# A fused four-part token kernel: products of the output experts turned round, factors spread over partitions by DMA, inverse roots by one power

## The reference, cut to what matters

```python
x = layernorm(x + A(x))   # Mamba block: conv over 4 taps, SSM over 4 heads, RMS norm, out_proj, LayerNorm
x = layernorm(x + B(x))   # attention of 8 heads; values and outputs come from one of 8 experts per head and token
x = layernorm(x + C(x))   # linear attention of 16 heads, gelu, rotary turn of q and k, LayerNorm
x = layernorm(x + D(x))   # soft mixture of 64 experts over all 4096 tokens
```

```python
values = einsum('bhne,ehdk,bnd->bhnk', gm, value_experts, x)
out    = einsum('bhij,bhjk->bhik', softmax(masked q k^T), values)
out    = einsum('bhne,ehkd,bhnk->bhnd', gm, output_experts, out).sum(heads)
```

## Time and profile before

| what | value |
|---|---|
| median of 3 runs | 1497.77 us (1497.28 to 1497.99) |
| profiled execution: its own time / its span | 1495.65 us / 1493.8 us |
| busy: TensorE (PE) / VectorE (DVE) / ScalarE (ACT) / GpSimd (POOL) | 1434.7 / 1205.2 / 820.6 / 748.6 us |
| mean granted TensorE clock | 0.98 |
| start of the first slot (block 2's `a_seg`) | 103.4 us |
| first instruction of D | 1005.5 us |

### The profile page before, as it was taken

The page is one execution under the profiler, slowest core; times in us unless marked ns, Lnnn a source line. Parts: engine busy times, 40 slices in busy tenths (PEclk is TensorE's granted clock), DMA queues, the critical chain, the costliest instruction groups (busy, mean ns, idle before and its releaser), DMA issues. The chain is left out here.

```text
span 1493.8 us, 32591 instructions
## 1 busy us (share of the span) xinstructions
PE 1434.7 (96%) x10940; PEld 1267.7 (85%) x10940; DVE 1205.2 (81%) x2359; ACT 820.6 (55%) x1850; POOL 748.6 (50%) x1833
## 2 busy tenths in 40 slices
PE   8789999999999999999999999988999999898998
PEld 6658888888888888888888887867999999898998
DVE  6778889889888898898898887768888888757664
ACT  4354555454555464455555544306776777667775
POOL 1433346346355354454453451226777777467772
PEclk8889999999999999999999999998999999999999
DMA  5100000000000000000000004007777777887872
GB/s 194 61 8 8 1 15 2 14 16 1 15 15 2 16 5 12 15 5 12 16 1 15 8 1 128 2 3 174 196 193 193 191 192 195 264 315 297 312 304 75
DMA packets 135426, 130.43 MB, mean 87 GB/s; under 512 B 7232, under 2 KB 125248, under 8 KB 128768
## 3 DMA queue, kind: packets, MB, share of 16 engines
q1 hardware_dynamic: 135296, 128.79, 27.9%
HBM read 72.93 MB, written 55.84 MB: 86 GB/s over the span
## 5 line engine op out<-in xcount | busy, mean ns | idle before, releaser
L737 PE MATMUL ps_l<-ve_f,oe 128*128 128x128 f32 x2048 | 275.7, 279 | 0.8 <-DVE ve_f L1740 0.8
L737 PEld LDWEIGHTS ps_l<-ve_f,oe 128*128 128x128 f32 x2048 | 248.8, 192 | 23.1 <-issue 20.4
L1740 DVE SCALAR_TENSOR_TENSOR ve_f<-ps_s,oT 128x512 f32<-128x512 f32 x248 | 166.7, 681 | 4.1 <-PE ps_l L737 2.3
L2934 POOL TENSOR_TENSOR d_s<-d_ex 128x1024 f32<-128x1024 f32 x31 | 125.2, 4040 | 83.0 <-ACT d_ex L2684 82.8
L1701 DVE COPY_PREDICATED vals<-oh,ps_l 128x1024 f32<-128x1024 int32 x112 | 146.9, 1312 | 19.3 <-PE ps_l L477 17.4
L2559 PE MATMUL ps_s<-d_ex,arena 128*128 128x128 f32 x1024 | 121.1, 277 | 4.6 <-DVE d_ex L2827 4.6
L2559 PEld LDWEIGHTS ps_s<-d_ex,arena 128*128 128x128 f32 x1024 | 118.2, 194 | 5.0 <-DVE d_ex L2827 5.0
L2547 PE MATMUL ps_l<-arena 128*128 (+1 forms) x960 | 114.5, 279 | 3.9 <-ACT d_raw L2679 3.9
L1293 ACT ACTIVATE ve_f<-ps_l,r 128x128 f32<-128x128 f32 x128 | 47.3, 370 | 125.9 <-DVE r L1713 125.6
L2547 PEld LDWEIGHTS ps_l<-arena 128*128 128x128 f32 x960 | 111.9, 195 | 4.1 <-ACT d_raw L2679 4.1
L475 PE MATMUL ps_l<-veH,x1H 128*128 128x512 f32 x256 | 115.2, 450 | 0.1
(11 more groups left out here) (332 smaller groups left out, 3842.7 us busy)
## 6 DMA issues: line engine op xcount, KB each, us to landing
logits<-d_raw SPq DMA_DIRECT2D x128, 256.0 KB, 3.5
e_lt<-logits SPq DMA_DIRECT2D x32, 1024.0 KB, 5.1
y_slots<-d_ys SPq DMA_DIRECT2D x64, 256.0 KB, 4.6
d_ex<-y_slots SPq DMA_DIRECT2D x8, 1024.0 KB, 6.9
e_y<-y_slots SPq DMA_DIRECT2D x6, 1024.0 KB, 7.2
d_w<-W SPq DMA_DIRECT2D x16, 256.0 KB, 3.4
arena<-xT SPq DMA_DIRECT2D x16, 128.0 KB, 2.4
arena<-x SPq DMA_DIRECT2D x16, 128.0 KB, 2.4
```

Source lines behind the costliest of these rows:

```text
L737: last = pe.matmul(ps_u[:, cols], oe[:, hp, e, :], mo[:, n % MO, hp, :], start=False, stop=(e == NE - 1 and hp == HP - 1), skip_group_chec ...
L1740: V.scalar_tensor_tensor(mo[:, n % MO, :, :].rearrange("p a n -> p (a n)"), chosen_of(b, c), float(NE - e), oT[:, u, c, :, :].rearrange("p ...
L2934: G.tensor_tensor(s8[:], part[:, 0:8, :], part[:, 8:16, :], ALU.add).then_inc(n, 1)
```

## The change

It rearranges B and C's turn and roots; D stays. In words: (1) the output product has `mo` as weights and `oe` as moving operand, so its sum has tokens on partitions, in `ps_m`, and `b_oa`, `b_oat` go; `b_start` becomes four products. (2) Expert numbers and factors of a block (32 values a token) are transposed once (`b_rnt`), copied (`b_rn`), stored to DRAM and read back spread over 64 partitions twice (`spread`); `b_choice`, `b_oht`, `b_rgs`, `b_rgb`, `b_ot` times factor go; ACT copies `ps_o` to `oT` twice a block, and one 128x1024 multiplication on DVE (`b_og`) puts the factors in. `b_mo` now reads the numbers from SBUF. (3) `c_rot` is two DMAs (`swap`) for blocks 0 to 12; the sign sits in `sinT`. (4) Roots on GpSimd are one scale-and-add and one power. (5) Scores of two head pairs are made at once in two PSUM tiles. (6) All engines' orders are new.

```diff
+def root(pool, wait_apart, done, k, source, var, eps, half, v, y):
+    wait_apart(pool, source)
+    pool.tensor_scalar(v[:], var, 1.0, eps, ALU.mult, ALU.add).then_inc(done, 1)
+    wait_apart(pool, (done, k + 1))
+    pool.tensor_tensor(y[:], v[:], half[:], ALU.pow).then_inc(done, RSQRT_OPS - 1)
...
+            def spread(b):
+                sp.wait_ge(q["b_rn"], b + 1)
+                wait(sp, q["b_nb"], 32 * (b - 1))
+                sp.dma_start(rn_dram[b % 2].rearrange("a r n -> (a r) n"), rows_s[0:4 * C * HP, :]
+                             ).then_inc(q["b_rn_out"], 16)
+                sp.wait_ge(q["b_rn_out"], 16 * (b + 1))
+                wait(sp, q["b_mo"], OUTS * b)
+                for a in range(2):
+                    sp.dma_start(nb[DH * a:DH * (a + 1), :, :, :, :].rearrange("p q c h n -> p (q c h n)"),
+                                 rn_dram[b % 2, a:a + 1].rearrange("a r n -> a (r n)").to_broadcast([DH, 2 * C * HP * P])
+                                 ).then_inc(q["b_nb"], 16)
+            def swap(b):
+                sp.wait_ge(q["c_q"], b + 1)
+                wait(sp, q["c_qr"], 2 * b)
+                sp.dma_start(t1[0:P:2, :, :], ql[1:P:2, :, :]).then_inc(q["c_swap"], 16)
+                sp.dma_start(t1[1:P:2, :, :], ql[0:P:2, :, :]).then_inc(q["c_swap"], 16)
...
                 for u in range(2):
+                    spread(2 * pair + u - 2)
                     load(2 * pair + u + 1, 1 - u)
+                    swap(2 * pair + u - 3)
                     store(2 * pair + u - 3)
...
                 for n in range(3):
                     sp.wait_ge(held_in[n], 16)
+            spread(Z)
...
+            def b_rnt(b):
+                pe.wait_ge(q["b_rg"], 2 * (b + 1))
+                wait(pe, q["c_x3t"], b - 1)
+                pe.transpose(mixed_home(b)[0:4 * C * HP, 0:P], mixed_of(b), id_f[:]).then_inc(q["b_rn_ps"], 1)
...
             def b_start(b, u):
-                wait(pe, q["b_v"], (NE - 1) * capped(b + 2))
-                pe.matmul(ps_u, id_r[:], x1H[:, u, :], start=True, stop=False, skip_group_check=True)
-                pe.matmul(ps_u, id_r[:], x1L[:, u, :], start=False, stop=False,
-                          skip_group_check=True).then_inc(q["b_start"], 1)
+                wait(pe, norms["lnB"]["rows"], C * b)
+                for c in range(C):
+                    cols = slice(c * P, (c + 1) * P)
+                    pe.matmul(sum_of(b)[:, cols], x1H[:, u, cols], id_r[:], start=(c == 0), stop=False,
+                              skip_group_check=True)
+                    last = pe.matmul(sum_of(b)[:, cols], x1L[:, u, cols], id_r[:], start=False, stop=False,
+                                     skip_group_check=True)
...
-                    last = pe.matmul(ps_u[:, cols], oe[:, hp, e, :], mo[:, n % MO, hp, :], start=False,
+                    last = pe.matmul(sum_of(b)[:, cols], mo[:, n % MO, hp, :], oe[:, hp, e, :], start=False,
...
+            def b_rn(b):
+                act.wait_ge(q["b_rn_ps"], b + 1)
+                wait(act, q["b_rn_out"], 16 * b)
+                copy(rows_s[0:4 * C * HP, :], mixed_home(b)[0:4 * C * HP, 0:P]).then_inc(q["b_rn"], 1)
+            def b_ot(b, u, g):
+                act.wait_ge(q["b_pv"], 2 * b + g + 1)
+                wait(act, q["b_mo"], OUTS * (b - 1))
+                copy(oT[:, u, :, 2 * g:2 * g + 2, :].rearrange("p c h n -> p h c n"),
+                     ps_o.rearrange("p (h c n) -> p h c n", h=2, c=C)).then_inc(q["b_ot"], 1)
...
+            def b_og(b, u):
+                dve.wait_ge(q["b_nb"], 32 * (b + 1))
+                dve.wait_ge(q["b_ot"], 2 * (b + 1))
+                V.tensor_tensor(oT[:, u, :, :, :], oT[:, u, :, :, :], nb[:, 0, :, :, :], ALU.mult).then_inc(q["b_og"], 1)
...
-                V.scalar_tensor_tensor(mo[:, n % MO, :, :].rearrange("p a n -> p (a n)"), chosen_of(b, c), float(NE - e),
+                V.scalar_tensor_tensor(mo[:, n % MO, :, :].rearrange("p a n -> p (a n)"),
+                                       nb[:, 1, c, :, :].rearrange("p a n -> p (a n)"), float(NE - e),
```

More of the change, by code:

```diff
@@ L329, in token_blocks @@
             a_op_ps a_r a_xb a_n a_x1t_ps a_x1h a_x1l a_x1
-            b_g_ps b_eg b_gate b_oht_ps b_oht b_qk_ps b_qk b_v_ps b_v0 b_v b_vg b_s_ps b_max b_p b_pt_ps b_pt
-            b_pv b_rg b_rgs b_rgb_ps b_rgb b_ot b_m_ps b_mo b_oe b_oa b_oat_ps b_x2t_ps b_x2t b_start
-            c_qk_ps c_g c_km c_q c_v_ps c_v c_rot_ps c_qr c_t2 c_krt_ps c_kr c_kv_ps c_kv c_out_ps c_z c_res c_n
+            b_g_ps b_eg b_gate b_qk_ps b_qk b_v_ps b_v0 b_v b_vg b_s_ps b_max b_p b_pt_ps b_pt
+            b_pv b_rg b_rn_ps b_rn b_rn_out b_nb b_ot b_og b_mo b_oe b_x2t_ps b_x2t b_start
+            c_qk_ps c_g c_km c_q c_v_ps c_v c_swap c_qr c_t2 c_krt_ps c_kr c_kv_ps c_kv c_out_ps c_z c_res c_n
             c_x3t_ps c_x3t c_x3""".split()
@@ L448, in _ @@
             sp.dma_start(oe[:], o_exp).then_inc(experts_in, 16)
-            for b in range(2, 5):
-                load(b, b % 2)
+            load(2, 0)
+            load(3, 1)
+            spread(0)
+            load(4, 0)
+            spread(1)
+            swap(0)
             store(0)
@@ L709, in b_choice @@
-            def b_choice(b, u, c):
-                if c == 0:
-                    pe.wait_ge(q["b_oht"], b + 1)
-                if (b, c) != (Z, 1):
-                    wait(pe, q["b_mo"], OUTS * b + NE * c)
-                else:
-                    wait(pe, q["b_pt"], HB * NB)
-                rows = slice(64 * c, 64 * c + 64)
-                for hp in range(HP):
-                    last = pe.matmul(chosen_of(b, c)[:, hp * P:(hp + 1) * P], pick[rows, hp, :, :].rearrange("p a k -> p (a k)"),
-                                     ohT[rows, u, :], start=True, stop=True, skip_group_check=True)
-                last.then_inc(q["b_m_ps"], 1)
@@ L1169, in _ @@
                     logits_ahead(k, i)
-            awake(ps_a, 14)
+            b_x2t(Y, 0)
+            c_qk(Y, 0)
+            b_start(Z, 1)
+            c_v(Y, 0)
+            b_out(Z, 0, 0)
+            b_out(Z, 0, 1)
+            c_rot(Y)
+            b_out(Z, 0, 2)
+            b_out(Z, 0, 3)
+            c_krt(Y)
+            b_out(Z, 0, 4)
+            b_out(Z, 0, 5)
+            c_kv(Y)
+            b_out(Z, 0, 6)
+            b_out(Z, 0, 7)
+            c_out(Y)
+            b_out(Z, 1, 0)
+            b_out(Z, 1, 1)
+            b_out(Z, 1, 2)
+            b_out(Z, 1, 3)
+            b_out(Z, 1, 4)
+            b_out(Z, 1, 5)
+            b_out(Z, 1, 6)
+            b_out(Z, 1, 7)
+            awake(ps_a, 20)
             b_x2t(Z, 1)
             c_qk(Z, 1)
-            awake(ps_a, 6)
+            c_x3t(Y)
+            for k in range(BK - 1):
+                logits_ahead(k, BB - 1)
             c_v(Z, 1)
@@ L2108, in _ @@
             b_v(1, 4)
-            b_mo(0, 0, 0, 1)
+            b_og(0, 0)
+            b_mo(0, 0, 0, 0)
             b_v(1, 5)
@@ L2157, in _ @@
             slot(NB // 2, 0, False, True, True, True, False)
+            b_res(Y)
+            b_x2(Y, 0)
+            b_og(Z, 1)
             b_mo(Z, 1, 0, 0)
@@ L2199, in _ @@
             G = nc.gpsimd
+            G.memset(half[:], -0.5)
             def a_am(b):
```

816 lines of the change are left out of this document (320 added, 496 removed).

## The result

The changed kernel takes **1442.09 us** (median of 4 runs, 1439.58 to 1445.82) against 1497.53 of the kernel before (4 runs); the ratio is 0.9634, 95% interval 0.9611 to 0.9658. I had forecast 1461, range 1444 to 1484: faster, as I said, but by 55 us where I had 37, and just outside the range. The profiled execution took 1441.11 us, with a span of 1439.4.

A forecast was written before the change was run, and what follows sets the result against it. PE was taken to bound the slots, latencies the head and tail. From 1495.65 us: slots 3 to 14 -29, slots 15 and 16 -5, head -8, tail +5, together -37, 1458.7; plus 2.1 for the median, 1461 us, range 1444 to 1484.

The forecast's parts named there:

- the sign: Whole kernel: forecast to become faster, chance 0.89, against 0.03 for the same and 0.08 for slower.
- 2.9 us priced for groups removed and added: PE in a slot: 3.1 us of factors, choice, `b_oht`, `b_oat` and `c_rot` leave, `b_rnt` comes; net 2.9 us off.
- the new wait of PE that I charged: PE in the values' section, through `b_og` and the spread's reads: 0.5 us of new idle a slot, bounds 0 and 2.
- slots 15, 16 and tail: End of the blocks before D: two slots save 2.4 us each, about 5, and the tail grows by 5, bounds 0 and +9.
- Two banks for scores and longer runs of `b_out`: PE's order within a slot: may save a few tenths of a us, counted as nothing.
- my rule: PE's groups: each priced by the distance from its first start to the next group's start, such as 0.33 us a choice.
- The head: Start to 158 us: 8 us less, from 3.1 for the root, 2 for block 1, 3 for block 0; bounds -13 and -2.
- "Nothing in the slots" for the roots: GpSimd's roots in the slots: they end long before their use, so shortening them frees GpSimd and nothing else.
- 1 (DVE the bound): Values' section: DVE becomes the bound, idle 1.5 to 2 us a slot instead of 0.5, about 1479 us; chance 0.16.
- 2 (late read): Spread's reads take 12.2 us, `b_og` 6 us late, 4 us a slot not absorbed, 1519 us; chance 0.08.
- 3 (GpSimd and DVE hold each other): Slots: DVE's two-SBUF-input work holds GpSimd, `a_mx` and `b_vg` slip 1 to 2 us, near 1475 us; chance 0.06.
- 4 (nothing waits, 1450): Whole kernel: no new idle, the clock holds, tail +2, 1450 us; chance 0.12.

## Why the prediction was right, and where it failed

**Right.** PE as the bound of the slots and the sign; 2.7 of the 2.9 us priced for groups removed and added; `b_rnt` 0.11 and `b_start` 0.58 us; the exchange of operands at nothing; `b_mo` at 0.69; no DVE wait for `ln2` in the head; 11.3 us from `b_rnt(Z)` to `b_out(Z)` (I had 10).

**Right by luck.** `b_og` at +12.2 us of the slot (I had +12.3): the reads go out at +5.0 and not +5.9, and last 7.2 us and not 5.1; the new wait of PE that I charged came in another place, at `b_out` for `b_mo`. And slots 15, 16 and tail at no change together: -8.3 and +8.4, where I had -5 and +5. In the tail the first 16 instructions of `b_out` ran at half speed, and `b_x2(Z)` came 34.1 us after the end of slot 16, where I had added up 30.4.

**The step that failed** is the sentence "Two banks for scores and longer runs of `b_out` may save PE a few tenths; I count nothing". It was not tenths but 1.7 us a slot by the account, 20 us in twelve slots. 0.97 of it is in scores, masks, turns and value products; 0.42 is in `a_seg` and `b_qk`, where the choice and `b_oat` had stood between them, so there my rule failed too, that a removed group gives back its own distance and no more. The runs put back 0.6 by the order of masks alone and 0.37 in the neighbours of the choice groups; which edit carries the rest stays open. Being unable to say how much, I should have put a bound on it instead of a zero. The slot of the earlier trace rows has the four score groups, 1.17 us each (mask, products, and what follows), of which this is one, and the 1.60 us from `a_seg` over the choice to the second product of `b_qk`:

```profile
526.41 0.38 PE L659 MATMUL ps_l<-negb,id_b 128*128 128x256 bf16 x2
526.73 0.49 PE L663 MATMUL ps_l<-qk 64*128 64x128 f32 x4
527.05 0.60 PE L667 MATMUL ps_l<-qk 64*128 64x256 f32 x4
527.58 1.13 PE L502 MATMUL ps_s<-arena,in_w 128*128 128x256 f32 x4
```
```profile
503.04 1.13 PE L529 MATMUL ps_s<-arena,low_s 128*128 128x512 f32 x2
504.10 0.39 PE L720 MATMUL ps_s<-ohT,pick 64*128 64x128 bf16 x4
504.42 0.38 PE L475 MATMUL ps_l<-x1H,wqH 128*128 128x256 f32 x1
504.64 0.29 PE L476 MATMUL ps_l<-x1L,wqH 128*128 128x256 f32 x1
```

The way from the last score product to another kind of group is 0.53 us there, and 0.43 in after's slot where the next scores follow. The second term mis-sized was the 0.5 us of new idle a slot: it was 0.13 in busy time, and against the usual slot length 0.24. Together: 12 x (-0.2 + 1.7 + 0.26) = 21 us, the whole miss of the slots. The head was over-forecast (-4.8 from block 1 on, -2.4 of it the roots, where I had -8), which hid a fifth of it.

**Smaller misses.** The power was to cost 0.3 us and costs 0.69; in the twelve slots nobody waits for it. DVE was to be busy for 48.7 us and is for 50.07, by `b_og` and `na` beside GpSimd.

**"Nothing in the slots" for the roots** failed as well, though it did not enter the sum: true for the waits of before, it overlooks that a short root moves what is queued behind it on GpSimd, and that the new order of DVE is only possible with it.

**Rivals.** 1 (DVE the bound) did not come, but came near: 94 per cent, and `b_out` standing behind DVE by some 0.6 us a slot. 2 (late read) did not come; its price was 9.4 us a slot for 7 us of lateness, not 4 for 6. 3 (GpSimd and DVE hold each other) is real and I had looked at one direction only: it is DVE that becomes slow, `qr` by 0.52 us, `b_og` by 0.5, the two `na` by 0.7. The Trainium skill (GPSIMD Engine Reference, Key points) says that GpSimd's SBUF access contends with DVE instructions that have two SBUF inputs; the traces agree, and show it in DVE's time too. In the kernel before with short roots it cost 1.07 us a slot. In the changed kernel it may cost up to 0.6: DVE runs without a pause from `na`, 0.7 us too long beside `b_vg`, to the very `b_mo` for which PE waits at 623.86 us. No run took that away. 4 (nothing waits, 1450) was nearest, and still 8 us short, for the same missing term.

## What to carry to other kernels

In a stretch where one engine never waits, price a removed group together with its neighbours: from the start of the group ahead to the second start behind it, with and without (added choice groups cost 1.17 us a slot, 0.80 by their own distances); and give a new order a range of its own, here 3 per cent. Ask of every shortened step on a side engine what it starts earlier, and beside whom. A wait of 6 us on TensorE cost 9 here, since the clock fell behind it; a hole that can't be closed is worth filling (21 products nobody reads brought 1.9 us). And look in the distances of starts for waits that a view doesn't count as idle: 0.64 us a slot of `b_out` was waiting, and 0.23 was shown.

## What was not expected of the hardware

- A 128x2 power on GpSimd takes 0.69 us (0.98 beside DVE), 3.5 times a multiplication of that shape; from the start of its scale-and-add to its end a root is 1.03 us.
- GpSimd and DVE side by side slow both: DVE's 128x512 two-input product 0.69 to 1.21 us, 128x1024 from 1.22 to 1.91, a 128x128 scaling with one tensor as input 0.34 to 0.70, GpSimd's 128x512 pair 2.04 to 2.49.
- A bf16 group of 64 rows behind a 512-column float product starts after 0.96 us, a float product after 0.46, and it costs 0.53 us where its own distance is 0.33.
- A float product of 128x128 is two instructions on PE and a float transpose one, which doubled one of my own test loads.
